# One block for two stages of a language-model tower kernel, fewer DMA issues, and three stores moved to the scalar engine's queue

## The chip, the cores and the metric

The kernel runs on one core of a Trainium2 chip. The metric is the device time of one execution in microseconds (us), as the median of several runs. The core has five instruction streams: TensorE (PE; its weight loads PEld), VectorE (DVE), ScalarE (ACT), GpSimd (POOL) and SyncE (SP). SP computes nothing; it issues transfers, each after the waits that stand before it. ACT and POOL can issue transfers too. All transfers run on the core's 16 DMA engines.

## What is computed

For B = 8 sequences of L = 512 tokens with D = 256 channels, the reference looks up embeddings and adds an attention layer and a mixture-of-experts layer:

```
h = onehot(x) @ embeddings
h = h + attn(layernorm(h))      # linear attention by a weighted delta rule, 16 heads of 16 channels
h = h + ffn(layernorm(h))       # router picks 2 of 8 experts, plus a shared expert

k, q, v = short_conv(x @ W + b, conv); k, q normalised by head; v = silu(v); beta = sigmoid(x @ Wbeta)
per chunk: T = tril(B K^T, -1); inv = (1 + T)^-1; U = inv (V - B W); W += K^T U
           O = Q W_avg * a + Q W * c + T_mat * (Q K^T) U
out = rmsnorm(O) @ Wout + bout
```

All types are float32. The kernel works with chunks of 32 tokens instead of the reference's 64, which gives the same result.

## The kernel before

The program has three stages, each with a block of its own in which every engine has its instruction list. At the end of a block all engines meet.

**First stage** (line 444, the page's 0 to about 597 us): a loop over the 8 sequences b. For each, PE projects and ACT and DVE apply the convolution: for n = 0 to 5, PE writes a bank (L575), ACT writes `cv` and `raw` (L695, L698), DVE adds three taps (L804). Then come the norms, K and Q, gram matrices and masked scores. The results go to DRAM: Q by channels (`qT_dram`, L471, 16 issues), K by tokens (`kk_dram`, L477, 4 issues), the gram matrix in two halves (`n_dram`, L482, 4 issues), beta K and V (`bv_dram`, L486), the scores (`sT_dram`, L494). The gram matrix is loaded back in another layout (`nx`, L491). DVE then inverts it by 62 half steps (L172, L175), laid between its work for the next two sequences, and SP stores the inverse in 8 issues (`store_inverse`, L184).

**Items.** There are 32 items, four tiles of 128 tokens for each sequence. An item goes through PE and ACT in four steps: `apply_inverse` (L288) gives Y and Z by channels, `turn_yz` (L299) turns them, `apply_scores` (L310) sums Y and Z with the scores, `turn_syz` (L320) turns the sums. POOL multiplies the queries by a table and adds the summed Y (`sum_queries`, L271, L276). In iteration b from 3 on, the first stage also works the items of sequence b - 3, placed by hand between its own PE and ACT instructions; so items 0 to 19 lie in the first stage. Items 20 to 31 lie in steps 0 to 3, 5 to 8 and 12 to 15 of the second stage.

SP moves the data of the items: `load_x` (the block-diagonal inverse `xbd`, 4 issues at L225, and `bv_i`, L227), `load_scores` (`sbd`, 4 issues at L234, and `q_i`, L238), `store_y` (L243), `store_rest` (Z and inner products, 4 issues at L251, and the queries, L254). `move_item(r)` issues them in this order:

```
load_x(sp, r + 1); store_y(sp, r); store_rest(sp, r - 1); load_scores(sp, r + 1)
```

`xbd`, `sbd` and `q_i` have one buffer each, so `load_x(r + 1)` waits until item r is solved, and `load_scores(r + 1)` until item r is scored and its queries are scaled.

**Second stage** (line 960, to about 915 us): 32 steps, each a chunk of four sequences. Each step loads Y, Z with inner products, K and queries (`load_step`: L978, L982, L987, L990, double buffered), keeps the state in PSUM, and ends in residual, layernorm, router scores and picks. u (L1155) is copied once in each step. POOL fills the residual rows `h` by gathers (L1012) over rows set to zero (L1019 for the first 4, L1023 for the rest). At its start SP loads weights and indices (L965), for which every other engine waits.

**Third stage** (to the end at 1516.8 us): the experts. The change leaves it as it is.

Of the kernel before, what the change touches and what calls it, by code (L numbers as in the profile page):

```python
# [6 lines left out]
P = 128  # L7
B, L, D = 8, 512, 256
H, DH = 16, 16
C = 32  # L10
# [95 lines left out]
def build(nc, ids, ids_lane, emb, wqkv, wbeta, wout, router, conv_w, qkv_b, bbeta, bout, rms, const, w_in, w_sw, w_out, out,  # L106
# [14 lines left out]
    with ExitStack() as top:  # L121
# [28 lines left out]
        s_nx = tail.enter_context(nc.semaphore("gram_loaded"))  # L150
        s_unit = tail.enter_context(nc.semaphore("unit_ready"))
        s_sub = tail.enter_context(nc.semaphore("vector_chain_inverse"))
        s_inv = tail.enter_context(nc.semaphore("inverse_ready"))
        s_xst = tail.enter_context(nc.semaphore("inverse_stored"))
# [33 lines left out]
        STORES = 16 * (16 + CH + 2)  # L188
# [14 lines left out]
        s_st = tail.enter_context(nc.semaphore("kv_stored"))  # L203
        s_x_in = tail.enter_context(nc.semaphore("item_x_loaded"))
        s_q_in = tail.enter_context(nc.semaphore("item_q_loaded"))
        s_s_in = tail.enter_context(nc.semaphore("item_scores_loaded"))
        s_bv_in, s_y_st, s_zo_st, s_qy_st = ([tail.enter_context(nc.semaphore(f"{n}{i}")) for i in range(2)]
                                                     for n in ("item_bv_loaded", "y_stored", "zo_stored", "queries_stored"))
        T = {n: tail.enter_context(nc.semaphore("item_" + n)) for n in (
# [19 lines left out]
        def load_scores(sp, r):  # L229
# [16 lines left out]
        def store_rest(sp, r):  # L246
            b, t, i = r // TILES, r % TILES, r % 2
            sp.wait_ge(T["z_ready"], r + 1)
            sp.wait_ge(T["inner_ready"], r + 1)
# [7 lines left out]
        def move_item(sp, r, more=True):  # L257
            if more:
                load_x(sp, r + 1)
            store_y(sp, r)  # L260
            if r:
                store_rest(sp, r - 1)
# [60 lines left out]
        def solved_out(act, r, bank):  # L323
# [4 lines left out]
            if r >= 2:  # L328
                act.wait_ge(s_y_st[r % 2], 16 * (r // 2))
            act.activation(y_out[r % 2][:].rearrange("p c n i -> p n c i"), bank[:].rearrange("p (n c i) -> p n c i", n=HQ, c=CH),  # L330
                           ACT.Copy, scale=table("keep_y")).then_inc(T["y_ready"], 1)

        def turned_out(act, r, bank):
# [4 lines left out]
            if r >= 2:  # L338
                act.wait_ge(s_zo_st[r % 2], 16 * CH * (r // 2))
# [17 lines left out]
        with ExitStack() as ctx:  # L357
# [41 lines left out]
            s_ids, s_w, s_zero = (sem(ctx, n) for n in ("ids_in", "weights_in", "h_zeroed"))  # L399
            s_emb = [sem(ctx, f"embedded{i}") for i in range(RING)]  # L400
            s_refill = sem(ctx, "h_refill_zeroed")
            s_pad = sem(ctx, "pad_zeroed")
            s_zero0 = sem(ctx, "zero_ready")
            s_slots = sem(ctx, "slots_zeroed")
            s_chain = sem(ctx, "vector_chain_a")
            s_xhat = sem(ctx, "xhat_ready")
# [1332 lines left out]
```

## Time and profile before

| | us |
|---|---|
| median of 3 runs | 1499.73 (1498.51 to 1503.61) |
| the profiled execution | 1518.6, its span 1516.8 |
| busy in the span: PE, DVE, ACT, POOL | 1179.7, 764.9, 515.8, 388.6 |
| mean granted TensorE clock | 0.874 of full speed |
| transfers of SP's queue | 202944 packets, 194.28 MB |

Busy times are sums over the whole span, over stages with different limits; an engine that is busy for half the span can still set the pace of one stage. The profiled execution is 18.9 us longer than the median.

### The profile page before, as it was taken

What the parts mean: (1) busy time and instruction counts of PE and PEld (TensorE: products, weight loads), DVE (VectorE), ACT (ScalarE), POOL (GpSimd) and SP (SyncE); (2) the same over time, 40 slices, a digit from 0 to 9 for tenths busy, and PEclk for the clock granted to TensorE, in tenths of its full rate; (3) what the DMA queues carried; (4) which work ended last, traced back from release to release, by engine and by line L of the source; (5) the groups of instructions that cost most, each with busy time, mean ns of one, the idle gap of its engine ahead of it and who ended that gap; (6) DMA issues with size and microseconds to landing.
All of it is one profiled execution on the core that took longest, in us unless ns stands there. A gap on an engine that the chain in (4) does not pass through costs nothing. (4 is left out here: it accounts for less than half of the span.)

```text
span 1516.8 us, 28805 instructions
## 1 busy us (share of the span) xinstructions
PE 1179.7 (78%) x10846; PEld 791.1 (52%) x10846; DVE 764.9 (50%) x1707; ACT 515.8 (34%) x1049; POOL 388.6 (26%) x366
## 2 busy tenths in 40 slices
PE   4766456566656561688697987999999999999997
PEld 2543334353535351466475764555666666666664
DVE  4599849586868683567646873221111212121211
ACT  3454245353636360433243332331122222222221
POOL 6100113131202021513226003662022222222222
PEclk9788679777878785867888997999999999999999
DMA  7644566868585968777687747953122323232322
GB/s 269 188 101 134 120 178 142 251 140 248 128 255 121 259 136 235 199 224 224 179 246 225 230 152 278 377 171 103 32 40 46 48 45 49 44 49 43 49 44 31
DMA packets 237366, 228.68 MB, mean 151 GB/s; under 512 B 88980, under 2 KB 177972, under 8 KB 236080
## 3 DMA queue, kind: packets, MB, share of 16 engines
q1 hardware_dynamic: 202944, 194.28, 45.3%
q0 software_dynamic: 16368, 19.96, 7.5%
q10 hardware_dynamic: 17920, 12.59, 2.8%
q8 instruction: 91, 1.49, 0.4%
q14 instruction: 43, 0.35, 0.1%
HBM read 117.39 MB, written 115.62 MB: 154 GB/s over the span
## 5 line engine op out<-in xcount | busy, mean ns | idle before, releaser
L1644 DVE TENSOR_TENSOR hid_all<-p_s,silu 128x512 f32<-128x512 f32 x103 | 71.3, 692 | 378.8 <-PE p_s L1495 249.7
L1694 POOL DMA_INDIRECT out_h<-y_sb,x_in x71 | 110.6, 1558 | 360.9 <-DVE y_sb L1656 343.0
L1552 ACT ACTIVATE silu<-p_m 128x512 f32<-128x512 f32 x103 | 61.5, 597 | 328.0 <-PE p_m L1488 223.4
L804 DVE SCALAR_TENSOR_TENSOR cv<-raw,conv_sb,cv 128x512 f32<-128x512 f32 x144 | 117.5, 820 | 83.6 <-ACT raw L698 81.7
L175 DVE TENSOR_TENSOR xt<-xt,prod 128x62 f32<-128x62 f32 (+15 forms) x248 | 142.0, 572 | 4.3
L172 DVE TENSOR_TENSOR prod<-nx,xt 128x62 f32<-128x62 f32 (+15 forms) x248 | 138.4, 558 | 2.5
L1510 PE MATMUL p_y<-wo,hid_all 128*128 x568 | 134.4, 379 | 0.8 <-ACT hid_all L1569 0.8
L1488 PE MATMUL p_m<-wi,xT_c 128*128 x284 | 133.5, 592 | 0.5 <-ACT xT_c L1565 0.5
L1495 PE MATMUL p_s<-ws,xT_c 128*128 x284 | 133.6, 593 | 0.0
L288 PE MATMUL p_item<-xbd,bv_i 128*32 128x128 f32 x1024 | 46.8, 340 | 108.4 <-issue 39.5
L575 PE MATMUL p_p<-xT,wqkv_sb 128*128 128x512 f32 x192 | 108.6, 705 | 0.7 <-issue 0.7
L1510 PEld LDWEIGHTS p_y<-wo,hid_all 128*128 128x128 f32 x568 | 102.5, 190 | 12.4 <-issue 1.4
L276 POOL TENSOR_TENSOR qy_out<-qy_out,sy_out 128x512 f32<-128x512 f32 x32 | 46.3, 1446 | 219.7 <-ACT sy_out L349 219.7
L271 POOL TENSOR_TENSOR qy_out<-q_i,cst_early 128x512 f32<-128x512 f32 x32 | 38.4, 1201 | 226.7 <-DMA q_i<-q_channels_dram 226.5
L288 PEld LDWEIGHTS p_item<-xbd,bv_i 128*32 128x32 f32 x1024 | 35.6, 135 | 116.7 <-issue 83.9
L629 PE MATMUL p_g<-kqM,kT 32*32 32x128 f32 x2048 | 52.8, 333 | 47.3 <-DVE h L874 26.4
L1684 POOL DMA_INDIRECT slots_in_dram<-rows,slot_of x64 | 62.2, 972 | 46.0 <-ACT rows L1560 31.5
L1488 PEld LDWEIGHTS p_m<-wi,xT_c 128*128 128x128 f32 x284 | 53.9, 190 | 38.4 <-issue 34.8
L1656 DVE COPY y_sb<-p_y 128x256 f32<-128x256 f32 x71 | 30.2, 425 | 85.5 <-PE p_y L1510 84.3
L629 PEld LDWEIGHTS p_g<-kqM,kT 32*32 32x32 f32 x2048 | 40.3, 121 | 59.0 <-issue 57.1
L1495 PEld LDWEIGHTS p_s<-ws,xT_c 128*128 128x128 f32 x284 | 48.5, 190 | 34.4 <-issue 34.4
L1453 PE MATMUL p_m<-xnT_c,wi 128*128 128x512 f32 x128 | 62.0, 608 | 5.3 <-DMA wo<-in_w_out 5.3
(155 smaller groups left out, 2093.9 us busy)
## 6 DMA issues: line engine op xcount, KB each, us to landing
slots_in_dram<-xt SPq DMA_DIRECT2D x18, 520.0 KB
x_in<-slots_in_dram SPq DMA_DIRECT2D x71, 130.0 KB, 2.1
q_channels_dram<-qT SPq DMA_DIRECT2D x128, 64.0 KB
k_tokens_dram<-h SPq DMA_DIRECT2D x32, 256.0 KB
chunk_gram_dram<-h SPq DMA_DIRECT2D x32, 256.0 KB
beta_kv_dram<-h SPq DMA_DIRECT2D x8, 1024.0 KB
nx<-chunk_gram_dram SPq DMA_DIRECT2D x8, 1024.0 KB, 6.3
scores_dram<-h SPq DMA_DIRECT2D x8, 1024.0 KB
```

The costliest lines, as they stand in the source:

```text
L172: ins = dve.tensor_tensor(pr, nx[b % 2][:, m, :, 0:m].rearrange("p e k -> p k e").unsqueeze(3).to_broadcast([P, m, 2, w]), xt[b % 2][:, m, ...
L175: ins = dve.tensor_tensor(kept, kept, pr, ALU.add)
L288: ins = pe.matmul(bank[C * f:C * f + C, n * P:(n + 1) * P], bv_i[r % 2][:, 4 * n + f, :], xbd[:, :, 4 * n + f, :], start=True, stop=True)
L575: ins = pe.matmul(p_p[n % 2][:], wqkv_sb[:, k, p, m * P:(m + 1) * P], xT[:, k, :], start=(k == 0), stop=(k == KH - 1))
L629: ins = pe.matmul(p_g[c * C:(c + 1) * C, g % 4, t % 2, g // 4, :], kT[r, g // 4, tok], kqM[r, g // 4, :, :, tok].rearrange("p w e i -> p ( ...
L804: ins = dve.scalar_tensor_tensor(cv[:, p, m, :], raw[:, p, m, j:j + L], conv_sb[:, p, m, j:j + 1], cv[:, p, m, :], ALU.mult, ALU.add)
L1488: ins = pe.matmul(p_m[n % 2][:], xT[s % 2][:, k, :], wi[:, e, k, :], start=(k == 0), stop=(k == KH - 1))
L1495: ins = pe.matmul(p_s[n % 2][:], xT[s % 2][:, k, :], ws[:, e, k, :], start=(k == 0), stop=(k == KH - 1))
L1510: ins = pe.matmul(p_y[s % 2][:, 0, :], hidT[s % 2][:, f * P:(f + 1) * P], wo[:, e, f, :], start=(f == 0), stop=(f == FK - 1))
L1644: dve.tensor_tensor(dst, p_s[n % 2][:], silu[n % 2][:], ALU.mult).then_inc(S["hid_ready"], 1)
L1684: pool.indirect_dma_start(xs_dram, bass.IndirectOffsetOnAxis(slot_of[:, t, k:k + 1], 0), rows[q][:, k, :], None).then_inc(s_scat[q], 16)
L1694: pool.indirect_dma_start(token_rows, bass.IndirectOffsetOnAxis(x_in[s % X_IN][:, D:D + 1].bitcast(U32), 0), y_sb[s % 2][:], None, compute ...
```

## The change

Five edits:

1. The two first stages share one block. The second stage's weights, indices and the loads of its steps 0 and 1 are issued by SP in the last iteration of the first stage (`start`). The other engines go from one stage into the next, each with waits of its own for what it overwrites. Banks and semaphores are laid out anew for this.
2. Q is stored in 8 issues instead of 16, K in 1 instead of 4, Z with the inner products in 1 instead of 4. The DRAM layouts of the three change with that: Q by head group and channel, K and Z by sequence and token.
3. Y and Z with inner products are stored by ACT, each right behind the ACT instruction that completes it.
4. SP's order changes: in an iteration from b = 2 on, the load of the inverse for the second item of the next iteration stands ahead of the load of `nx` and the store of the scores; the loads for item 0 stand in the middle of iteration 2 instead of at its end.
5. ACT waits for the stores of K alone before it overwrites K, not for all stores of the sequence.

```diff
-    qT_dram = nc.dram_tensor("q_channels_dram", [B, TILES, P, HQ, P], F32, kind="Internal").ap()
-    kk_dram = nc.dram_tensor("k_tokens_dram", [NC_BATCH, B, C, 2 * D], F32, kind="Internal").ap()
+    qT_dram = nc.dram_tensor("q_channels_dram", [B, HQ, P, L], F32, kind="Internal").ap()
+    kk_dram = nc.dram_tensor("k_tokens_dram", [B, L, 2 * D], F32, kind="Internal").ap()
-    zo_dram = nc.dram_tensor("z_and_inner_dram", [NC_BATCH, B, C, 2 * D], F32, kind="Internal").ap()
+    zo_dram = nc.dram_tensor("z_and_inner_dram", [B, L, 2 * D], F32, kind="Internal").ap()
...
-            sp.dma_start(q_i[:], qT_dram[b, t]).then_inc(s_q_in, 16)
+            sp.dma_start(q_i[:], qT_dram[b, :, :, t * P:(t + 1) * P].rearrange("n p l -> p n l")).then_inc(s_q_in, 16)
-        def store_y(sp, r):
+        def store_y(act, r):
-            sp.wait_ge(T["y_ready"], r + 1)
-            sp.dma_start(y_dram[b // GROUP, t * CH:(t + 1) * CH, :, b % GROUP].rearrange("c p x -> p c x"),
+            act.wait_ge(T["y_ready"], r + 1)
+            act.dma_start(y_dram[b // GROUP, t * CH:(t + 1) * CH, :, b % GROUP].rearrange("c p x -> p c x"),
...
-            for c in range(CH):
-                sp.dma_start(zo_dram[t * CH + c, b], zo_out[i][tok(c)].rearrange("p w h d -> p (w h d)")
-                             ).then_inc(s_zo_st[i], 16)
+            act.dma_start(zo_dram[b, t * P:(t + 1) * P], zo_out[i][:].rearrange("p w h d -> p (w h d)")).then_inc(s_zo_st[i], 16)
...
                         if b >= AHEAD:
-                            move_item(sp, r)
+                        if r:
+                            store_queries(sp, r - 1)
+                        load_scores(sp, r + 1)
                             move_item(sp, r + 1)
...
-                        for f in range(4):
-                            for m in range(2):
+                    for n in range(HQ):
                                 for w in range(2):
-                                    sp.dma_start(qT_dram[b, :, f * C + w * DH:f * C + (w + 1) * DH, m::2].rearrange("t d n l -> d n t l"),
-                                                 qT[m * 4 * DH + f * DH:m * 4 * DH + (f + 1) * DH].rearrange("d n (t l) -> d n t l", t=TILES)
-                                                 ).then_inc(s_st, 16)
+                            sp.dma_start(qT_dram[b, n].rearrange("(f w d) l -> w f d l", w=2, d=DH)[w],
+                                         qT[n % 2 * 4 * DH:(n % 2 + 1) * 4 * DH, n // 2]).then_inc(s_st, 16)
...
+                        if half == 0 and b == B - 1:
+                            start_next(sp)
+                        if half == 0 and b == AHEAD - 1:
+                            load_x(sp, 0)
+                            load_scores(sp, 0)
...
+                    if AHEAD - 1 <= b < B - 1:
+                        load_x(sp, r + 5)
                         sp.wait_ge(s_ngst, 64 * (b + 1))
...
                         if b:
-                            act.wait_ge(s_st, b * STORES)
+                        act.wait_ge(s_kst, b * K_STORES)
...
+            def start(sp):
+                sp.wait_ge(first["s_cv"], 6 * B)
                     for dst, src in ((wout_in[:], wout), (router_sb[:], router), (rms_sb[:], rms), (bout_sb[:], bout),
...
+                load_step(sp, 0)
+                load_step(sp, 1)
...
                         sp.dma_start(zo[i][:].rearrange("p w d -> p (w d)"),
-                                     zo_dram[c, b:b + GROUP].rearrange("b i x -> (b i) x")).then_inc(s_zo[i], 16)
+                             zo_dram[b:b + GROUP, c * C:(c + 1) * C]).then_inc(s_zo[i], 16)
...
                             sp.dma_start(kk[i][:].rearrange("p n x -> p (n x)"),
-                                         kk_dram[c, b:b + GROUP].rearrange("b i x -> (b i) x")).then_inc(s_kk[i], 16)
+                                 kk_dram[b:b + GROUP, c * C:(c + 1) * C]).then_inc(s_kk[i], 16)
...
+                pool.wait_ge(s_kst, K_STORES * B)
+                pool.wait_ge(first["s_bv"], 4 * B)
                     pool.memset(h[:, 0:4], 0.0).then_inc(s_hz, 1)
...
+                pool.wait_ge(s_st, STORES * B)
+                pool.wait_ge(first["s_ngst"], 64 * B)
                     pool.memset(h[:, 4:], 0.0).then_inc(s_hz, 1)
...
+                    if s == 0:
+                        pe.wait_ge(first["s_sT"], TILES * B)
                         pe.wait_ge(s_kk[s % 2], 16 * k_loads(s))
```

How SP's list moves, from the store of beta K and V in the iteration of b = 6 on. Each row is an issue (line, destination <- source, the shape of the destination); `h` is the space in which the first stage keeps K, the gram matrix and the scores. Before:

```order
L486 DMA beta_kv_dram<-h 128x4x512
L225 DMA xbd<-chunk_inverse_dram 32x512 x4
L227 DMA bv_i<-beta_kv_dram 128x512
L243 DMA y_channels_dram<-y_out 128x4x128
L251 DMA z_and_inner_dram<-zo_out 32x512 x4
L254 DMA queries_dram<-qy_out 128x4x128
L234 DMA sbd<-scores_dram 32x512 x4
L238 DMA q_i<-q_channels_dram 128x512
L482 DMA chunk_gram_dram<-h 128x8x64 x2
L491 DMA nx<-chunk_gram_dram 128x2048
L494 DMA scores_dram<-h 128x4x512
L225 DMA xbd<-chunk_inverse_dram 32x512 x4
```

In the changed program, from the same store on:

```order
L492 DMA beta_kv_dram<-h 128x4x512
L227 DMA xbd<-chunk_inverse_dram 32x512 x4
L229 DMA bv_i<-beta_kv_dram 128x512
L257 DMA queries_dram<-qy_out 128x4x128
L236 DMA sbd<-scores_dram 32x512 x4
L240 DMA q_i<-q_channels_dram 128x4x128
L483 DMA chunk_gram_dram<-h 128x8x64 x2
L227 DMA xbd<-chunk_inverse_dram 32x512 x4
L229 DMA bv_i<-beta_kv_dram 128x512
L499 DMA nx<-chunk_gram_dram 128x2048
L502 DMA scores_dram<-h 128x4x512
L257 DMA queries_dram<-qy_out 128x4x128
```

The issues for Y and Z are gone, and the second load of `xbd` stands ahead of `nx` and the scores. Earlier in the same iteration the Q stores (L471, in the changed program L474) go from 16 rows with the destination shape 32x4x128 to 8 with 4x16x512.

SP's list in the last iteration of the first stage, in the changed program; the two stages' transfers are now mixed, and K's and Z's loads walk a source of 4 sequences by 32 tokens by 512 numbers:

```order
L966 DMA ids_lane_sb<-in_ids_lane 128x32
L986 DMA zo<-z_and_inner_dram 128x1x512
L992 DMA kk_b<-k_tokens_dram 128x1x512
L982 DMA yy<-y_channels_dram 128x512
L986 DMA zo<-z_and_inner_dram 128x1x512
L992 DMA kk_b<-k_tokens_dram 128x1x512
L995 DMA qq<-queries_dram 128x512
L492 DMA beta_kv_dram<-h 128x4x512
L227 DMA xbd<-chunk_inverse_dram 32x512 x4
L229 DMA bv_i<-beta_kv_dram 128x512
```

Before, the same loads stood behind the end of the block:

```order
L494 DMA scores_dram<-h 128x4x512
L444 UNCONDITIONAL_BRANCH
L961 UNCONDITIONAL_BRANCH
L965 DMA wout_in<-in_wout 128x512
L965 DMA router_sb<-in_router 128x16
L965 DMA rms_sb<-in_rms 128x1
L965 DMA bout_sb<-in_bout 128x256
L965 DMA ids_lane_sb<-in_ids_lane 128x32
L982 DMA zo<-z_and_inner_dram 128x512
L987 DMA kk_b<-k_tokens_dram 128x512
L978 DMA yy<-y_channels_dram 128x512
L982 DMA zo<-z_and_inner_dram 128x512
```

ACT's list at the end of an item, around the start of the convolution of the next sequence. Before:

```order
L346 COPY syz_ch<-p_item 128x512
L349 ACTIVATE sy_out<-p_item,cst_early 128x4x4x32
L354 COPY zo_out<-p_item 128x256
L695 ACTIVATE cv<-p_p,now_b,conv_sb 128x512
L698 ACTIVATE raw<-p_p,qkvb_sb 128x512
```

In the changed program:

```order
L349 COPY syz_ch<-p_item 128x512
L352 ACTIVATE sy_out<-p_item,cst_early 128x4x4x32
L357 COPY zo_out<-p_item 128x256
L252 DMA z_and_inner_dram<-zo_out 128x512
L696 ACTIVATE cv<-p_p,now_b,conv_sb 128x512
```

A store, with a wait for the copy just before it, now stands between the item's last copy and the first output of the convolution.

## Rows read from the trace of the kernel before

**Rows 1.** Windows by stage: us, busy (xinstructions) per engine, clock, DMA share, GB/s

```profile
170.00:252.00 82.00, 43.39 (x639) 31.08 (x638) 60.47 (x117) 36.15 (x65) 9.74 (x7) 0.79 0.61 157
...
484.00:562.00 78.00, 47.94 (x706) 34.86 (x704) 60.72 (x108) 39.02 (x72) 12.71 (x11) 0.82 0.76 192
...
562.00:602.00 40.00, 5.07 (x132) 3.73 (x132) 19.80 (x31) 0.75 (x2) 4.40 (x5) 0.52 0.80 213
...
602.00:761.00 159.00, 115.82 (x1866) 88.97 (x1866) 102.21 (x259) 50.73 (x125) 56.68 (x49) 0.75 0.73 211
...
761.00:803.00 42.00, 37.30 (x676) 29.39 (x675) 18.69 (x70) 21.19 (x53) 14.06 (x14) 0.91 0.81 243
```

**Rows 2.** Waits in order of total, DVE, 170 to 605: total, times, longest

```profile
DVE cv L804 <- ACT raw L698: 71.3, 13, 17.6
...
DVE wout_sb L1236 <- DMA ids_lane_sb<-in_ids_lane: 19.8, 1, 19.8
```

**Rows 3.** Waits, PE, 170 to 610

```profile
PE p_item L288 <- issue: 38.5, 4, 14.1
...
PE p_item L288 <- DMA xbd<-chunk_inverse_dram: 31.4, 4, 8.5
...
PE p_item L288 <- DMA bv_i<-beta_kv_dram: 25.7, 2, 24.5
```

**Rows 4.** Timeline of the last two batches, SP: start, us, issue, [idle <-releaser]

```profile
480.29 11.07 SPq L471 DMA_DIRECT2D q_channels_dram<-qT  x16
...
497.74 0.98 SPq L486 DMA_DIRECT2D beta_kv_dram<-h  x1
...
498.84 3.22 SPq L225 DMA_DIRECT2D xbd<-chunk_inverse_dram  x4
...
512.77 0.46 SPq L494 DMA_DIRECT2D scores_dram<-h  x1
...
513.34 2.11 SPq L225 DMA_DIRECT2D xbd<-chunk_inverse_dram  x4
```

**Rows 5.** Timeline of the last batch, PE and DVE

```profile
505.26 1.94 PE L288 MATMUL p_item<-xbd,bv_i 128*32 128x128 f32 x32 [7.76 <-issue]
...
523.11 1.94 PE L288 MATMUL p_item<-xbd,bv_i 128*32 128x128 f32 x32 [7.41 <-DMA xbd<-chunk_inverse_dram]
...
529.11 0.75 DVE L804 SCALAR_TENSOR_TENSOR cv<-raw,conv_sb,cv 128x512 f32<-128x512 f32 x1 [9.19 <-ACT raw L698]
```

**Rows 6.** Timeline, issues of SP and ACT for an item

```profile
503.10 1.87 SPq L251 DMA_DIRECT2D z_and_inner_dram<-zo_out  x4
...
683.83 0.52 ACTq L1197 DMA_DIRECT2D ffn_input_channels_dram<-xnT  x1
```

**Rows 7.** Timeline of the change of stage, DVE, SP, PE, POOL

```profile
580.20 0.69 DVE L874 TENSOR_TENSOR h<-p_g,cst_early 128x512 f32<-128x512 f32 x1
...
587.91 0.43 SPq L494 DMA_DIRECT2D scores_dram<-h  x1
...
597.06 0.36 SPq L965 DMA_DIRECT2D wout_in<-in_wout  x1
...
602.54 1.19 PE L1040 MATMUL p_u_turn_x<-zo,cst 128*128 128x256 f32 x2 [31.48 <-DMA zo<-z_and_inner_dram]
...
607.91 6.10 POOL L1023 MEMSET h<- 128x7168 f32 x1
...
617.14 0.34 SPq L238 DMA_DIRECT2D q_i<-q_channels_dram  x1
```

**Rows 8.** Timeline of step 3, PE

```profile
646.58 1.93 PE L288 MATMUL p_item<-xbd,bv_i 128*32 128x128 f32 x32 [11.21 <-DMA bv_i<-beta_kv_dram]
```

**Rows 9.** Window of ten late steps, columns as in rows 1

```profile
835.00:893.00 58.00, 55.55 (x1112) 42.20 (x1100) 47.24 (x179) 18.59 (x60) 0.00 (x0) 1.00 0.72 225
```

**Rows 10.** Page, part 2: GB/s in 40 slices

```profile
GB/s 269 188 101 134 120 178 142 251 140 248 128 255 121 259 136 235 199 224 224 179 246 225 230 152 278 377 171 103 32 40 46 48 45 49 44 49 43 49 44 31
```

**Rows 11.** Instructions of L1155, 835 to 900

```profile
L1155 ACT COPY u<-p_u_turn_x x12: 372/373/374, 835.4 to 899.6; 128x256 f32<-128x256 f32 x12
```

More of the change, by code:

```diff
@@ L887, in build @@
-        with ExitStack() as ctx:
+                        if half == 0:
+                            sp.wait_ge(s_bv, b * 4 + 4)
+                            sp.dma_start(bv_dram[b].rearrange("(t p) x -> p t x", p=P),
+                                         bv[:].rearrange("p t h w d -> p t (h w d)")).then_inc(s_st, 16)
+                            if b >= AHEAD:
+                                move_item(sp, r + 3)
+                    if AHEAD - 1 <= b < B - 1:
+                        load_x(sp, r + 5)
@@ new lines, in sync @@
+            def sync(sp):
+                for s in range(NT):
+                    if s >= 2:
+                        load_step(sp, s)
+                    if s == 3:
+                        store_inverse(sp, B - 2)
+                    if s - 1 in item_in:
+                        r = item_in[s - 1]
+                        move_item(sp, r, more=r + 1 < ITEMS and r != BREAK)
+                    if s == 11:
+                        store_inverse(sp, B - 1)
+                        load_x(sp, BREAK + 1)
+                        load_scores(sp, BREAK + 1)
+                    if s == step_of[ITEMS - 1] + 2:
+                        store_queries(sp, ITEMS - 1)
@@ new lines, in gpsimd, with gather, add_bias @@
+            def gpsimd(pool):
+                pool.wait_ge(s_weights, 16 * 5)
+                def gather(n):
+                    pool.indirect_dma_start(h[:, n, :], None, emb, bass.IndirectOffsetOnAxis(ids_sb[:, n:n + 1].bitcast(U32), 0),
+                                            bounds_check=VOCAB - 1, oob_is_err=False).then_inc(s_lane[n % 4], 16)
+                def add_bias(n):
+                    pool.wait_ge(s_lane[n % 4], 16 * (n // 4 + 1))
+                    pool.tensor_tensor(h[:, n, :], h[:, n, :], bout_sb[:], ALU.add).then_inc(s_hb, 1)
+                pool.wait_ge(s_kst, K_STORES * B)
+                pool.wait_ge(first["s_bv"], 4 * B)
+                pool.memset(h[:, 0:4], 0.0).then_inc(s_hz, 1)
+                pool.wait_ge(s_hz, 1)
+                for n in range(4):
+                    gather(n)
+                pool.wait_ge(s_st, STORES * B)
+                pool.wait_ge(first["s_ngst"], 64 * B)
+                pool.memset(h[:, 4:], 0.0).then_inc(s_hz, 1)
+                pool.wait_ge(s_hz, 2)
+                for n in range(NT):
+                    add_bias(n)
+                    if n + 4 < NT:
+                        gather(n + 4)
+                    if n in item_in:
+                        sum_queries(pool, item_in[n])
@@ L960, in build @@
+            return dict(start=start, sync=sync, gpsimd=gpsimd, tensor=tensor, scalar=scalar, vector=vector)
+        with ExitStack() as ctx:
+            first = first_stage(ctx)
+        with ExitStack() as ctx:
+            second = second_stage(ctx)
             with nc.Block() as block:
@@ L993, in _ @@
-                    for s in range(NT):
-                        load_step(s)
-                        if s == 3:
-                            store_inverse(sp, B - 2)
-                        if s - 1 in item_in:
-                            r = item_in[s - 1]
-                            move_item(sp, r, more=r + 1 < ITEMS and r != BREAK)
-                        if s == 11:
-                            store_inverse(sp, B - 1)
-                            load_x(sp, BREAK + 1)
-                            load_scores(sp, BREAK + 1)
-                        if s == step_of[ITEMS - 1] + 2:
-                            store_rest(sp, ITEMS - 1)
+                    first["sync"](sp, second["start"])
@@ L1149, in _ @@
+                    first["tensor"](pe)
+                    second["tensor"](pe)
                 @block.scalar
                 def _(act):
[L1151 to L1161 removed]
@@ L1226, in _ @@
-                    store_xnT(NT - 1)
-                    for i in range(2):
-                        act.wait_ge(s_xn_out[i], 16 * (NT // 2))
-                        act.wait_ge(s_xnT_out[i], 16 * (NT // 2))
+                    first["scalar"](act)
+                    second["scalar"](act)
                 @block.vector
                 def _(dve):
-                    link = Chain(dve, S["chain"], -1)
-                    dve.wait_ge(s_weights, 16 * 5)
-                    for k in range(KH):
-                        dve.tensor_scalar(wout_sb[:, k, :], wout_in[:, k, :], rms_sb[:, 0:1], None, ALU.mult).then_inc(s_wout, 1)
@@ L1338, in build @@
+                    second["vector"](dve)
         tail.close()
```

1544 lines of the change are left out of this document (769 added, 775 removed).

## The prediction, written before the result was known

> **What bounds the kernel now.** I read the windows by stage first, then the waits, then the timeline at the waits found. In the last full batch of the first stage DVE is busy 60.7 of 78 us, PE 47.9 [rows 1]. So DVE sets the pace there where it has work. The list of DVE's waits says when it has none: 71.3 us in front of the taps for ACT's `raw`, in 13 places, 17.6 us of it once [rows 2]. ACT is late because PE stands still in front of `apply_inverse`: 38.5, 31.4 and 25.7 us, by name behind `xbd` and `bv_i` [rows 3]. So a load of an item holds PE, PE holds ACT, and ACT holds DVE.
>
> The timeline of SP shows why these loads are late. For item 16, SP spends 11.07 us on the 16 Q stores, stores beta K and V at 497.74 and comes to `xbd` at 498.84. For item 17 it comes to `xbd` at 513.34, behind 1 MB of `nx` and 1 MB of scores [rows 4]. PE gets the first at 505.26 after 7.76 us and the second only at 523.11, after 7.41 us; DVE then stands 9.19 us [rows 5].
>
> At the change of stage DVE has its last masked scores at 580.9 and next works at 601.2, for the weights (19.8 us) [rows 2, 7]. PE stands 31.48 us. POOL sets `h` to zero only from 607.91, and SP, which has to wait until POOL has scaled the first item's queries behind that, comes to the next loads at 617.14 [rows 7]. From there SP issues nearly without a pause to the `xbd` of step 3, for which PE waits to 646.58 [rows 8]. The late steps are PE's: 55.6 of 58 us [rows 9].
>
> **The change, part by part.** All terms are against the profiled execution, 1518.6 us.
>
> *Loads of items earlier.* The loads of item 0 move from behind the scores of b = 2 to the middle of that batch; that takes nearly all of the 17.6 us away. For the later batches I take item 17. PE would have been free at 523.11 - 7.41 = 515.7, and `xbd`, now issued behind the gram matrix alone, some 6 us earlier, has landed by then. DVE's tap follows `apply_inverse` by 529.11 - 523.11 = 6 us, so it comes at 521.7; DVE has been free since 519.9. Of 9.19 us, 1.8 remain [rows 5]. The load of item 16 waits for DVE's beta K as before (L486, then L225) and gains under 1 us; about 2 us a batch of small waits behind it stay. Left over five batches: 5 x 3.8 = 19 us of the 71.3, so 52 saved. The merged Q, K and Z issues shorten SP's list, by 11.07 / 2 for Q and 1.87 x 3/4 for each Z [rows 4, 6], but at the Q stores SP then only waits for DVE's beta K: nothing more.
>
> *Y and Z on ACT.* An issue with many rows took ACT 0.52 us and SP 1.87 / 4 = 0.47 [rows 6]; the wait for ACT's own copy in front of it adds one or two tenths. Of 8 such in a batch I count two on the way to a `raw`: 5 x 1.2 = 6 us against. In the second stage they lie in ACT's idle time. Behind an issuing ACT waits the next `cv`, and for that DVE. Under a full queue an issue took 3.22 / 4 = 0.8 us [rows 4]; that end is in the last rival.
>
> *One block.* PE and DVE can go on at 581 instead of 602: the first half of step 0 moves by 24 us. But the second half of POOL's zeroing still waits for the scores' landing, and SP waits for POOL. The scores go out at 587.91, and SP comes to the weights at 597.06 [rows 7]; POOL can so start at 597 rather than at 607.91. SP's list is shorter, which brings the scores forward by some 3 us, but four large loads of the second stage now stand in front of them and take this back, and a little more. Since everything up to 646.58 hangs on that chain, I count 10 us, not 24; bounds 6 and 18.
>
> *Merged transfers.* The bytes are the same. Their shape is not: the Q stores have an outermost count of 4, and so has the source of the loads of Z and K in the second stage (4 sequences). No transfer of the kernel before has one under 16. I take it that a transfer is dealt out over the 16 DMA engines by its outermost entries; then these 64 stores and 62 loads run on 4 engines each, and if always on the same ones, these carry the stage. No row shows this, so both ends are priced. If 16 engines share as before, the term is 0. On four engines:
>
> - Late steps, 58 us for ten: 225 GB/s x 5.8 us = 1.31 MB each [rows 9]. Two loads (0.52 MB) on four engines and the rest on 16 give 131 + 49 = 180 KB to a loaded engine. An engine moves 225 / 16 / 0.72 = 19.5 GB/s while busy [rows 9]; in the best slice 377 / 16 = 23.6 [rows 10]. So a step needs 9.2 or 7.6 us, not 5.8. Their packets are of the better kind, so 8.2: 12 steps from 835 on [rows 11] x 2.4 = 29 us (22 to 41).
> - Steps 12 to 15, 42 us: 2.55 MB each, 258 KB to a loaded engine, 10.9 to 13.8 us at 23.6 and 18.8 GB/s [rows 1]. I take 13.2 against 10.5: 11 us (2 to 13).
> - Steps 0 to 11, 159 us: 2.80 MB each, 273 KB, 11.6 to 15.1 us against 13.25 [rows 1]: 8 us (0 to 22). Steps 16 to 19: 2 us (0 to 4).
> - First stage: a batch keeps an engine busy 0.76 x 78 = 59 us, at 192 / 16 / 0.76 = 15.8 GB/s [rows 1]. The Q stores, 1.05 MB, add 196 KB to a loaded engine, 8.3 to 12.4 us: 68 to 72. The batch after the first term is about 69 us, so this just fits or costs up to 3: 4 us in all.
>
> The Trainium skill ("DMA: Bandwidth & Descriptors", section "Why a DMA increments its semaphore by 16 and not by 1") states a rule of this kind: the number of engines is the largest one up to 16 that divides the slowest count of both sides, and these are always the lowest-numbered. By it the sum below holds; with 16 engines the same sum would be about -65. No run here shows it yet.
>
> Sum: -52 + 6 + 4 = -42 for the first stage, -10 for the change of stage, +50 for the second: **-2 us**, 1516.6 in the profiled execution. The median stands at 1499.73 / 1518.6 = 0.9876 of it: **1498 us**.
>
> **The rivals.**
>
> 1. *Faster, 16 engines for every shape.* For it: every row so far moves at a rate of all engines. Against it: four outermost entries can't be dealt to 16 without cutting them. Then first stage -46, change of stage -18, second 0 or a little less: -65, 1453.6, so 1435.
> 2. *Faster, four engines that keep up.* The low ends: the loaded engines run at 23.6 GB/s, since their packets are of 2 KB. First stage -46, change -14, second +24: -36, so 1463.
> 3. *Slower, the loads of Z and K in the second stage bind.* Place: L986 and L992. At 18 to 19.5 GB/s the late steps take 9.2 us, the steps with items 13.8 and 15.1: +80. In the first stage the loaded engines are full, loads of items queue behind Q stores, and only 30 of its gain stay; 6 remain at the change. +44, so 1543. It decides as soon as the second stage loses over 52 us, with the late steps over 8.3 us.
> 4. *Slower, ACT's stores.* At 0.8 us each plus the wait, and all 64 on the way, 45 us more than counted: 1543. Against it: ACT is busy half of the first stage's batch.
>
> **How the numbers follow.** A measurement tells about 0.3% (4.5 us) from no change. Forecast 0.40, rival 1 0.13, rival 2 0.20, rival 3 0.22, rival 4 0.05. The forecast's own terms spread by some 18 us about 1498, which gives faster 0.16, within 0.3% 0.11, slower 0.13. Faster: 0.13 + 0.20 + 0.16 = 0.49; the same: 0.11; slower: 0.22 + 0.05 + 0.13 = 0.40. The range has to reach both sides, to 1436 and 1542; it leaves out half of rival 1 and the upper half of rivals 3 and 4. The forecast's own range is 1475 to 1520.
>
> **What would show it.** In the profile after: DVE's wait for `raw` at about 20 instead of 71 us, none of them over 4; a batch of 69 to 71 us; PE's gap at the change of stage under 12 us, and SP's `q_i` of item 21 some 10 us earlier against the end of the first stage. Packets of Q stores must be 2 KB, and a late step must take about 8.2 us with PE waiting for `zo` or `kk_b`. Late steps of 5.8 us mean rival 1, and the second stage's gain is then 18; of over 8.5 us, rival 3. If the waits in front of `apply_inverse` remain at 7 us, my first term is wrong. A long busy stretch of ACT's queue between item copies and `cv` means rival 4.

## The result, and the profile after

The changed kernel is **slower**: four runs gave 1512.7, 1517.6, 1519.7 and 1527.1 us, median 1518.64, against 1501.67 for the kernel before; the ratio is 1.0109 with a 95% interval of 1.0076 to 1.0142. One of the four runs of the kernel before took 1864.11 us and is left out of the ratio; the median of the other three is the 1499.73 of the first table. By the medians of four that is 17 us more, about 1%, where 1498 was forecast. The time lies in the stated range, but the likeliest case had the wrong side.

The profiled execution of after took 1512.7 us (the shortest of the four), its span 1510.2. Against the 1518.6 us of the first profile of the kernel before it looks faster. So the kernel before was profiled a second time (experiment b0, 1503.5 us). The table sets all three side by side. The first stage's end is the end of DVE's last masked scores (L874), the next four columns are starts of u (L1155 before, L1166 after), the last is the rest of the execution's time.

| us | end of first stage | u of step 4 | step 12 | step 20 | last (31) | behind it |
|---|---|---|---|---|---|---|
| before, first profile | 580.9 | 659.6 | 760.9 | 835.4 | 899.6 | 619.0 |
| before, second (b0) | 576.6 | 655.3 | 751.6 | 819.4 | 885.8 | 617.7 |
| after | 538.2 | 626.2 | 726.4 | 811.1 | 894.3 | 618.4 |
| after less b0, by part | -38.4 | +9.3 | +3.9 | +16.9 | +16.8 | +0.7 |

The first stage gives back 38 us, everything behind it takes 48. Against the first profile the same parts are -42.7, +9.3, -1.1, +10.2, +19.0 and -0.6, together -5.9. Two stretches of that execution are long. One is the start: ACT's first `xT` copy of b = 3, before any item is worked, comes at 170.4 us in the first profile, at 159.1 in b0 and at 159.2 in after. So 11.2 of the 42.7 us lie ahead of b = 3, where b0 and after are alike, and are not the change's; from that copy to the end of the first stage it is 410.4 us in the first profile, 417.5 in b0 and 378.9 in after, a gain of 31.5 or 38.6. The other is steps 12 to 20, 74.5 us against b0's 67.8, where the change costs.

**The first stage.** The list of waits of after, DVE, 170 to 605 us (total, times, longest):

```profile
DVE norm L836 <- ACT norm L723: 17.8, 5, 5.0
DVE cv L804 <- ACT raw L699: 17.5, 13, 3.6
```

The wait for `raw` was 71.3 us with a longest of 17.6 [rows 2]; it is 17.5 now, none over 3.6. A wait for `norm` (8.0 us before) has grown. Why is not shown: it is 16.0 in f3, which has SP's old order, 15.7 in f2, which stores Y and Z from SP, and 8.1 in g1, which has neither the one block nor the merged stores. The waits of PE for an item (170 to 610 us) beside those of [rows 3]:

```profile
PE p_item L290 <- DMA xbd<-chunk_inverse_dram: 41.3, 5, 13.2
...
PE p_item L290 <- issue: 7.9, 1, 7.9
...
PE p_item L290 <- DMA bv_i<-beta_kv_dram: 5.2, 2, 3.0
```

95.6 us have become 54.4, and the 13.2 among them lie in the first step of the second stage.

**The change of stage.** SP's timeline of after (start, us, issue):

```profile
537.87 2.59 SPq L995 DMA_DIRECT2D qq<-queries_dram  x1
540.50 0.52 SPq L492 DMA_DIRECT2D beta_kv_dram<-h  x1
541.14 4.29 SPq L227 DMA_DIRECT2D xbd<-chunk_inverse_dram  x4
...
546.42 4.16 SPq L236 DMA_DIRECT2D sbd<-scores_dram  x4
...
551.09 3.84 SPq L483 DMA_DIRECT2D chunk_gram_dram<-h  x2
558.73 0.35 SPq L499 DMA_DIRECT2D nx<-chunk_gram_dram  x1
559.14 0.44 SPq L502 DMA_DIRECT2D scores_dram<-h  x1
...
563.94 1.72 SPq L236 DMA_DIRECT2D sbd<-scores_dram  x4
577.02 0.38 SPq L240 DMA_DIRECT2D q_i<-q_channels_dram  x1
```

and POOL's:

```profile
567.82 6.07 POOL L1033 MEMSET h<- 128x7168 f32 x1 [24.58 <-DMA scores_dram<-h]
...
575.90 1.10 POOL L273 TENSOR_TENSOR qy_out<-q_i,cst_early 128x512 f32<-128x512 f32 x1
```

The scores are issued at 559.14, 21 us behind DVE's end; before it was 7 us behind (587.91 against 580.9 [rows 7]). POOL waits for their landing to 567.82, 30 us behind that end. Before it was 27, though the scores went out so much earlier: POOL then came to this point only behind the change of block, the weights and four gathers. SP stands from 565.7 to 577.0 for the queries that POOL scales next. PE starts step 0 at 540.5, 62 us earlier than before, and then waits: u of steps 0 to 4 took 55.8 us before and takes 84.4.

**The late steps.** The window of eleven late steps of after; columns as in [rows 9], which answers to it (us, busy of PE, PEld, DVE, ACT, POOL, granted clock, DMA share, GB/s):

```profile
811.00:894.00 83.00, 71.83 (x1235) 52.53 (x1232) 53.58 (x198) 21.18 (x66) 0.00 (x0) 0.88 0.52 168
```

A step takes 7.6 us on the mean (83.2 / 11), not 5.8, and the DMA engines are busy 52% on the mean over all 16, not 72%. The waits of ACT and PE in that window:

```profile
ACT xnT L1204 <- DMA ffn_input_channels_dram<-xnT: 13.5, 7, 2.6
```

```profile
PE p_u_turn_x L1049 <- ACT xnT L1204: 8.9, 7, 1.9
```

In this window PE never waits for `zo` or `kk_b` themselves. ACT waits to overwrite `xnT`, whose store is behind, and PE for ACT; PE's idle time is 11 us of 83. The granted clock is 0.88 where it was 1.00, so the matmuls are also slower (PE is busy 6.5 us in a step, and was 5.6).

### The profile page after: what moved, and what is told of

Read it like the earlier page. It is cut to its first block and busy times, and to the rows that moved or that the text cites. A ratio compares the mean times of both kernels' runs of the same rounds, so it can differ in the third digit from the quotient of the medians.

```text
span 1510.2 us, 28640 instructions
## 1 busy us (share of the span) xinstructions
PE 1194.3 (79%) x10846; PEld 803.2 (53%) x10846; DVE 767.6 (51%) x1707; ACT 518.1 (34%) x1049; POOL 391.4 (26%) x366
## 5 line engine op out<-in xcount | busy, mean ns | idle before, releaser
L1686 DVE TENSOR_TENSOR hid_all<-p_s,silu 128x512 f32<-128x512 f32 x103 | 71.3, 692 | 378.3 <-PE p_s L1537 249.7
L172 DVE TENSOR_TENSOR prod<-nx,xt 128x62 f32<-128x62 f32 (+15 forms) x248 | 141.5, 570 | 2.5
L577 PE MATMUL p_p<-xT,wqkv_sb 128*128 128x512 f32 x192 | 104.2, 681 | 0.7 <-ACT xT L691 0.7
L290 PE MATMUL p_item<-xbd,bv_i 128*32 128x128 f32 x1024 | 43.0, 320 | 64.2 <-DMA xbd<-chunk_inverse_dram 43.3
L273 POOL TENSOR_TENSOR qy_out<-q_i,cst_early 128x512 f32<-128x512 f32 x32 | 42.1, 1314 | 187.3 <-DMA q_i<-q_channels_dram 187.2
L1530 PEld LDWEIGHTS p_m<-wi,xT_c 128*128 128x128 f32 x284 | 53.9, 190 | 38.4 <-issue 34.8
L290 PEld LDWEIGHTS p_item<-xbd,bv_i 128*32 128x32 f32 x1024 | 32.5, 127 | 72.6 <-DMA xbd<-chunk_inverse_dram 49.3
```

What stands on the lines that cost most here:

```text
L172: ins = dve.tensor_tensor(pr, nx[b % 2][:, m, :, 0:m].rearrange("p e k -> p k e").unsqueeze(3).to_broadcast([P, m, 2, w]), xt[b % 2][:, m, ...
L290: ins = pe.matmul(bank[C * f:C * f + C, n * P:(n + 1) * P], bv_i[r % 2][:, 4 * n + f, :], xbd[:, :, 4 * n + f, :], start=True, stop=True)
L577: ins = pe.matmul(p_p[n % 2][:], wqkv_sb[:, k, p, m * P:(m + 1) * P], xT[:, k, :], start=(k == 0), stop=(k == KH - 1))
L1530: ins = pe.matmul(p_m[n % 2][:], xT[s % 2][:, k, :], wi[:, e, k, :], start=(k == 0), stop=(k == KH - 1))
L1686: dve.tensor_tensor(dst, p_s[n % 2][:], silu[n % 2][:], ALU.mult).then_inc(S["hid_ready"], 1)
```

## Experiments

All ratios are to the kernel before, run on the same chip; its median was 1505.01 us beside b0 to e3, 1515.27 beside f1 to f4 and 1515.02 beside g1 to g4. So kernels of different groups are compared by their ratios. f2, f3 and f4 are edits of e1, which was not run beside them; f1 stands in for it there. g3 and g4, the same two kernels as e1 and f1 on one chip, differ by 1 us.

### b0: the kernel before, profiled again

> The kernel before, unchanged, profiled again. The profile that the prediction used took 1518.6 us where the timed runs took 1498.5 to 1503.6. Theory A: that execution was a long one by chance and a second profile comes near 1500 us; then the sum has to be made against 1500, and the comparison of the two profiles (1518.6 and 1512.7) hides some 19 us of loss. Theory B: a profiled execution of this kernel is always about 19 us longer, then it comes to 1515 to 1522 again and the ratio to the other runs of before is 1.000 within 0.003.

Measured: 1505.18, ratio 1.0007 (0.9986 to 1.0028), the profiled execution 1503.5 us. Theory B falls: a profiled execution is not longer as such. The first profile is long by 4.3 us in the first stage (11.3 at the start, 7.0 of them back behind it) and by 9.5 from step 4 to 31 (table above). That it was so by chance, as theory A has it, is not shown. The same kernel has medians of 1515.27 and 1515.02 us on two other chips, with single runs up to 1520.65. The first `xT` copy of b = 3 comes at 169.5 to 171.9 us in all eight profiles taken there, as in the first profile, and at 159.1 to 161.4 in those of b0, e1, e2 and e3. So the first profile looks like one of another chip; on which it was taken is not on record.

### e1: loads of Z and K as four loads of one sequence

```
-                sp.dma_start(zo[i][:]..., zo_dram[b:b + GROUP, c * C:(c + 1) * C]).then_inc(s_zo[i], 16)
+                for n in range(GROUP):
+                    sp.dma_start(zo[i][lane(n)]..., zo_dram[b + n, c * C:(c + 1) * C]).then_inc(s_zo[i], 16)
```

and the same for `kk`; PE waits for 16 * GROUP.

> The changed kernel, with each load of Z and of K for the second stage as four loads of one sequence (32 rows) instead of one with an outermost count of 4; 186 more issues of SP. Theory (these 62 loads run on four DMA engines and carry the second stage): late steps go from 7.2 us and more back to 5.8, the second stage from first to last u goes from 352 to 300 to 315 us, and the time to 1470 to 1485. Rival (the second stage is long for SP's order, the stores from ACT or the early start): late steps stay over 7 us and the time at 1510 to 1525, or goes up for the added issues.

Measured: 1477.03 us, ratio 0.9833 (0.9786 to 0.9879). Against the changed kernel's 1.0109 that is 2.8%, some 41 us less, for 186 more issues. The window of late steps in e1, then its DMA issues in that window (KB each, median us from issue to landing), then those of after, 811 to 894 us:

```profile
790.00:855.00 65.00, 61.75 (x1237) 47.40 (x1237) 53.71 (x202) 20.80 (x67) 0.47 (x1) 1.00 0.72 215
```

```profile
qq<-queries_dram SPq DMA_DIRECT2D x11, 256.0 KB, 3.7
yy<-y_channels_dram SPq DMA_DIRECT2D x10, 256.0 KB, 3.8
...
ffn_input_channels_dram<-xnT ACTq DMA_DIRECT2D x11, 128.0 KB, 3.3
```

```profile
yy<-y_channels_dram SPq DMA_DIRECT2D x10, 256.0 KB, 6.7
...
qq<-queries_dram SPq DMA_DIRECT2D x10, 256.0 KB, 9.2
...
ffn_input_channels_dram<-xnT ACTq DMA_DIRECT2D x11, 128.0 KB, 7.1
```

The late steps are back at 5.8 to 5.9 us (64.6 for eleven), the clock at 1.00. The transfers shown are the same in both kernels, and none has an outermost count of 4. They land in about half the time once the loads of Z and K are dealt out. The reading: a transfer over all engines has landed only when the last of them is done, and in after four of them are busy with Z and K.

### g1: the kernel before, with only the memory order of Z and K changed

```
-    kk_dram = ...("k_tokens_dram", [NC_BATCH, B, C, 2 * D], ...)
-    zo_dram = ...("z_and_inner_dram", [NC_BATCH, B, C, 2 * D], ...)
+    kk_dram = ...("k_tokens_dram", [B, L, 2 * D], ...)
+    zo_dram = ...("z_and_inner_dram", [B, L, 2 * D], ...)
```

Stores and loads use the new addresses, in the same number of issues.

> The kernel before, with the order of Z and of K in memory as the change has it (sequence, then token), and nothing else: the same issues, bytes and packets, but the 62 loads of the second stage walk a source of 4 x 32 x 512, where before it was one run of 128 rows. Theory (by that shape they run on four DMA engines): the load increments its semaphore 4 times and not 16 times, late steps go from 5.8 to 7.0 us and more, and the time rises by 30 to 45 us over the kernel before. Rival (in the changed kernel something else made the steps long): within 5 us of the kernel before.

Measured: 1548.02 us, ratio 1.024 (1.017 to 1.0309): 36 us (26 to 47) from the memory order alone. The page's row of SP's queue (packets, MB, share), first of the kernel before (b0), then of g1:

```profile
q1 hardware_dynamic: 202944, 194.28, 46.0%
```

```profile
q1 hardware_dynamic: 202200, 194.28, 44.2%
```

The bytes are the same; 744 packets are gone, which is 62 loads x 12. (The expectation had said "the same packets".) The semaphore events in the traces tell what they were. In b0 a Z load has 16 events from the DMA side (508 on record for 32 loads), in g1 5 (151 for 32; some are missing), in the late steps one within 1.0 us of the issue and four late. The Z load issued at 855.83 has them at 856.77 and at 864.38 to 864.77. So four engines report a landing where 16 did.

The packets show that these are the same four engines for Z and K. While a Z and a K load of one step are both on their way (from 1.5 us behind the K load's issue to Z's landing, 63 us in all between 845 and 925), exactly four packets are in flight in 31% of the time; on eight engines it would mostly be eight or more. Over the whole late window it is 31% in g1 and 26% in after (811 to 894), against 1% in b0 (820 to 885) and 2% in e1. A Z load lands after 9.0 us (median) and a K load after 11.3, where b0 has 2.7 and 3.6; in after it is 6.7 and 9.3.

The late steps take 6.2 to 8.1 us, 7.3 on the mean. This is the cleanest proof: nothing of the order, the blocks or the queues differs. The place in memory does differ, but e1 reads the same places with 16 engines and has late steps of 5.9 us.

### e2 and e3: the Q stores on 16 engines

e2 gives the changed kernel the 16 Q stores of before (partitions outermost, pieces of 512 B) and the Q layout that goes with them; e3 is e1 and e2 together.

> The changed kernel, with the Q stores alone as before: 16 issues of 512 B pieces in a batch, partitions outermost. Theory (four engines for the Q stores cost the first stage little): the batch stays at 70 to 73 us, the time within 6 us of 1518.6. Rival (the four-engine Q stores hold up the items' loads behind them): the batch falls to 68 us or less, the waits for xbd go from 41 us to under 25, and the time falls by 12 us or more.

> Both edits, so no transfer has an outermost count of 4. Theory: the gain of the loads and that of the Q stores add up, 1468 to 1485 us. If the four-engine shapes were no matter, 1510 to 1530.

Measured: e2 1515.11 us, ratio 1.0072 (1.0035 to 1.011); e3 1476.55, ratio 0.9805 (0.9773 to 0.9838). e3 and e1 differ by 0.5 us in their medians and by 0.3% in their ratios, e2 and after by 0.4% in their ratios; the intervals overlap in both pairs. So the Q stores on four engines cost 0 to 6 us. The batches of e2 do not become shorter (70.9 to 75.2 us, 69.9 to 73.5 in after). Its waits for `xbd` fall as the rival said, from 41.3 to 22.0 us, but the wait of the same instruction that is named "issue" grows from 7.9 to 23.6. Whether the gains of e1 and e2 add up is within the noise.

### f3: SP's order of before, in e1

The lines that move `load_x(r + 5)` ahead of `nx` and item 0 to the middle of b = 2 are taken back.

> e1, with SP's order of the kernel before: the x of a batch's first item loaded at the start of its own batch, behind nx and the scores of the last, and the loads of item 0 behind the scores of b = 2. One block, ACT's stores and the merged stores stay. Theory (the first stage's gain of 42 us comes from the order): DVE's waits for raw are back at 65 to 75 us, and the time rises by 35 to 50 us, to 1512 to 1527. Rival (fewer issues or ACT's stores made the loads early): it rises by under 20 us.

Measured: 1524.22 us, ratio 1.0051 (1.0029 to 1.0072), against 0.9834 for f1 on that chip: 33 us by the ratios, 35 by the medians. The first stage ends at 579.5 us, and DVE's waits (170 to 590 us) show why:

```profile
DVE cv L800 <- ACT raw L695: 62.7, 15, 16.2
DVE norm L832 <- ACT norm L719: 16.0, 5, 4.6
```

The order alone makes the gain of the first stage. It was expected at 35 to 50 us and is just at or under the lower edge. Without it one block, merged stores and ACT's queue, with every load on 16 engines, leave a kernel 0.5% slower than before.

### f2: Y and Z stored from SP again, in e1

```
     def move_item(sp, r, more=True):
...
+            store_y(sp, r)
             if r:
+                store_zo(sp, r - 1)
                 store_queries(sp, r - 1)
```

> e1, with the stores of Y and of Z and inner products (one issue each) put back into SP's queue, where the kernel before had them. Theory (the stores from ACT cost the first stage 6 to 10 us, seen as DVE's wait for norm of 18 instead of 8 us): that wait is back at 8 us and the time falls by 4 to 9 us, to about 1470. Rival (they relieve SP, whose list sets when item loads go out): the waits for xbd grow and the time rises by 5 us or more.

Measured: 1494.53 us, ratio 0.9851 (0.9819 to 0.9884), beside 0.9834 (0.9803 to 0.9864) for f1. Its waits of DVE:

```profile
DVE cv L806 <- ACT raw L701: 30.7, 15, 4.1
...
DVE norm L838 <- ACT norm L725: 15.7, 5, 4.5
```

The theory falls: the wait for `norm` hardly changes (17.0 in f1), so ACT's issues do not make it, and the wait for `raw` is 8 us longer than f1's 22.4. The time is 5.8 us over f1's by the medians and 0.2% by the ratios, whose intervals overlap. So the stores from ACT cost nothing that can be measured and may gain a little.

### f4: the early start taken away, in e1

`start_next(sp)` moves from the middle of b = 7 to behind its scores.

> e1, with the early start taken away: SP issues the second stage's weights and the loads of steps 0 and 1 behind the scores of the last batch. Theory (the early start is worth nothing, since POOL waits for the scores, which its 24 issues hold up): u of step 0 comes 15 to 20 us later, that of step 4 within 4 us of e1's, the time within 5 us of 1477. Rival (the early start is worth the 24 us by which step 0 moves): 1495 or more.

Measured: 1493.13 us, ratio 0.9861 (0.983 to 0.9893). u of step 0 comes at 565.2, 18 us behind the first stage's end (547.4), where in e1 both fall together; yet u of step 4 comes 79.6 us behind that end, in e1 81.2. The time is 4.4 us over f1's by the medians. The intervals overlap and leave room for about 11: the early start of step 0, 24 us by the prediction's count, is worth 4 us or nothing, at most some 11.

The same run shows what holds the scores up. Their issue in f4, where the first stage ends at 547.4, and then in e1, where it ends at 541.8:

```profile
551.77 0.43 SPq L500 DMA_DIRECT2D scores_dram<-h  x1
```

```profile
559.69 0.43 SPq L502 DMA_DIRECT2D scores_dram<-h  x1
```

That is 4.4 and 17.9 us behind that end. So the issues of the next stage in front of them cost the scores some 13 us.

### f1, g3, g4, g2: POOL's wait for the scores

f1 lets POOL zero lanes 0 to 7 first (the K quarter of `h`) and wait for the scores only at lane 4:

```
-                pool.memset(h[:, 0:4], 0.0).then_inc(s_hz, 1)
+                pool.memset(h[:, 0:8], 0.0).then_inc(s_hz, 1)
...
                 for n in range(NT):
                     add_bias(n)
+                    if n == 4:
+                        pool.wait_ge(s_st, STORES * B)
+                        pool.wait_ge(first["s_ngst"], 64 * B)
+                        pool.memset(h[:, 8:], 0.0).then_inc(s_hz, 1)
+                        pool.wait_ge(s_hz, 2)
```

g4 is f1 again, g3 is e1 again, and g2 is f1 with K in memory as before, so that each K load is one issue on 16 engines.

> e1, with POOL's order at the change of stage alone altered: its first memset takes the K quarter of h (lanes 0 to 7), and the wait for the scores with the memset of the rest stands behind the sums of the first items, at lane 4. In e1 SP stands from 566.2 to 578.5 us for POOL's scaled queries, which stand behind that wait. Theory (the chain scores, POOL, SP takes back what the early start gives): SP's stand of 12 us goes, the time from DVE's last masked scores to the u of step 4 falls from 82 to under 72 us, and the time from 1477 to 1463 to 1470. Rival (the DMA engines are full there, or xbd is late by its own chain): 1472 to 1480.

> e1 again, on the chip of g1, g2 and g4: 0.983 of the kernel before, as in its first run (0.9786 to 0.9879).

> f1 again, beside e1 on one chip. In f1's trace the time from DVE's last masked scores to the u of step 4 was 74.5 us, in e1's 81.9, but the two ran on different chips. Theory: 4 to 8 us under g3. Rival: the steps behind give it back, within 3 us of g3.

> e1 with POOL's order of f1, and K in memory as before (four stores in a batch, each load of a step one issue on 16 engines again): 90 issues of SP fewer in the second stage and 24 more in the first. Theory (SP's list is part of the chain of the early steps, and f1's edit is worth 7 us to step 4): the fastest of all, 5 to 12 us under g3. Rival (DMA engines are full there and the issues are hidden): within 4 us of g3.

Measured: f1 1488.76, ratio 0.9834 (0.9803 to 0.9864); g3 1488.21, 0.982 (0.9765 to 0.9875); g4 1487.23, 0.9828 (0.9771 to 0.9884); g2 1483.55, 0.9805 (0.9756 to 0.9854). SP's stand of 12 us is gone in f1:

```profile
563.92 0.34 SPq L499 DMA_DIRECT2D nx<-chunk_gram_dram  x1
564.30 0.43 SPq L502 DMA_DIRECT2D scores_dram<-h  x1
...
568.55 2.43 SPq L236 DMA_DIRECT2D sbd<-scores_dram  x4
571.02 0.44 SPq L240 DMA_DIRECT2D q_i<-q_channels_dram  x1
```

and the time does not move. What the edit gives up to step 4 goes by step 12 (from the first stage's end):

| | to step 4 | to step 12 | step 12 to 31 |
|---|---|---|---|
| before, two profiles | 78.7, 78.7 | 180.0, 175.0 | 138.7, 134.2 |
| g3 (e1) | 82.8 | 177.9 | 140.2 |
| g4 (f1) | 71.6 | 176.5 | 142.4 |
| f4 (late start) | 79.6 | 179.6 | 140.0 |
| after | 88.0 | 188.2 | 167.9 |
| g1 | 81.3 | 186.0 | 158.4 |

With the loads on 16 engines step 12 comes 175 to 181 us behind the first stage's end in ten of the eleven profiles there are, whatever the first steps do (170.5 in g2's). g4 is 1 us under g3, so the rival of f1 and g4 holds. What binds in between was not taken apart. The trace shows only that PE waits 10 to 13 us for `zo` of step 12 in g3, g4 and after (9.7 and 10.0 before, too), and that SP has issued `chunk_inverse_dram` of the last sequence (L184, 8.2 to 8.9 us) and a further item's loads in front of it.

One kernel's profiles differ here by as much as the edits do: from step 12 to 31 e1 took 132.9 us and g3, the same kernel, 140.2; the difference lies in steps 12 to 20 (68.3 and 76.1), for steps 20 to 31 take 64 to 65 us in every profile with the loads on 16 engines but b0's (66.4).

g2 is faster than both kernels, 1.95% under before. Its lead over e1 is 5 us beside g3 and within the intervals, between its theory (5 to 12) and its rival (within 4); e3 has the same ratio. Its step 12, some 7 us earlier than elsewhere with fewer issues of SP, speaks for the theory, but it is one profile.

## Why the prediction was right and wrong

**The first stage: mechanism right, size 4 to 10 us too good.** -42 was forecast for it. It is -42.7 against the profile that was used, but 11.2 of this lie ahead of the batches with items, so the agreement is luck: the batches gave 31.5 us against that profile and 38.6 against b0, and f3 puts the order at 33 to 35. DVE's wait for `raw` was to fall to about 20 us with none over 4, and is 17.5 with 3.6; a batch was to take 69 to 71 us, and takes 70 to 74 (ACT's `xT` copies, L691, start at 159.2, 232.7, 304.6, 377.9 and 447.8). f3 shows that it is the order. Of the 17.6 us at the first batch with items, of which nearly all was to go, the batch gained 8.1 (81.6 to 73.5). Of the two costs against it, ACT's +6 was not there (f2), and the Q stores' +4 is within 0 to 6 (e2). The wait for `norm`, which the prediction did not have, took 10 us back.

**The change of stage: the step that failed.** "I count 10 us, not 24; bounds 6 and 18". It cost 9.3 us. The mechanism was named: SP's large loads in front of the scores take back what its shorter list gives, "and a little more". That term was put at next to nothing, and it measured 14 us: the scores went out 20.9 instead of 7.0 us behind DVE's end. The 11 issues of the next stage took SP from 530.04 to 540.50, 10 us, and the item's `xbd` and `sbd` and the second half of the gram matrix behind them took it 12.3 us instead of 6.2; f4 shows that moving the next stage's issues back gives 13 us. So the 11 us by which POOL was to start sooner were gone, and 3 more. PE's gap at the step was 14.4 us and not under 12, and SP's `q_i` of item 21, expected 10 us earlier against the end of the first stage, came 38.8 us behind it, where it had been 36.2. The bounds left a loss out without a reason for it. Not all of the 9.3 is SP's order: with the loads on 16 engines u of step 4 comes 80.3 to 83.0 us behind the end (e1, e3, f2, f3, g3), 2 to 4 us later than before and not 9.3, so the rest seems to belong to the shape of the loads. Of that the prediction had about 3 us here, four twelfths of its +8 for steps 0 to 11, so it stood at -7 for this part and not at -10. The split is rough, for e2 has that shape and 83.7. And f4, f1 and g4 show more: up to step 12 an early start or a shorter chain gave nothing that can be measured, so the lower bound of 6 was hardly to be had either.

**The second stage: mechanism right, sizes off on the lighter side.** The transfers with an outermost count of 4 run on four engines; g1's 12 missing packets and four late semaphore events for each load show the count, and e1 and g1 the price in the whole time: 41 and 36 us. By the rule of the Trainium skill ("DMA: Bandwidth & Descriptors", section "Why a DMA increments its semaphore by 16 and not by 1"), the largest number up to 16 that divides the slowest count of both sides, 4 is what should come, and the trace agrees. That it is always the same engines, the lowest-numbered, that section of the Trainium skill also states. The traces have no engine's number, but Z and K share theirs (four packets in flight with both loads on their way, in 31% of that time in g1), and transfers over all engines land in 6.7 and 9.2 instead of 3.8 and 3.7 us. Term by term (forecast; against the profile used; against b0): late steps +29; 19.0; 16.8. Steps 12 to 19 +13; 10.2; 16.9. Steps 0 to 11 +8; -1.1; 3.9 for steps 4 to 11. So +50 was 28 or 38 from step 4 on. A late step took 7.6 us, the lower of the two prices worked out. By the prediction's estimate of 180 KB a step, a loaded engine then moves 180 KB / 7.6 us = 23.7 GB/s, the rate of the profile's best slice [rows 10]. 8.2, between the two, was taken; the rate to take was that of an engine without a gap. And the waiting engine was not the one named: not PE for `zo`, but ACT for its own store, which shares the engines.

**The sum.** -42 - 10 + 50 = -2 was forecast. Against the profile that was used the parts are -42.7 + 9.3 + 28.1, with -0.6 behind them: -5.9, which looks near, and would be +5.3 without the 11.2 at the start. Against b0 they are -38.4 + 9.3 + 37.6 + 0.7 = +9.2. The medians say +17: after's own profile is its shortest run, 5.9 us under its median, and b0's is 1.8 over the median of before (9.2 + 5.9 + 1.8 = 16.9). So against b0 the first stage was 4 us too good, the change of stage 19 too good, and the second stage 12 too dear; the last hid part of the others. The ratio 0.9876 of median to profile was laid over all parts alike, but b0 shows no such ratio: of the first profile's 15 us, 11 lie at the start and 10 between steps 4 and 31, and 7 come back in between. It made the forecast look sound against the profile. The sign came from the change of stage: with the 9.3 measured there in place of -10 the prediction's own sum is +17.

**The rivals.** 1 and 4 are out (16 engines by g1's count; ACT's stores by f2). 2, four engines that keep up, had the right price for the late steps, and 3 named the right side, slower, but by a price of +80 in the second stage that no run shows. What happened is a fifth case: the forecast's mechanisms, with a change of stage that costs instead of giving.

## What to carry to other kernels

Before two issues are merged into one, look at the outermost count of both sides: one issue with a count of 4 cost this kernel more than three further issues of SP do, and its price shows at other transfers too, as late landings on queues that were not touched. An earlier start of a stage is worth only what the last release on its way allows; move it alone (f4) before it is counted. And profile the kernel before again beside the runs that it is compared with: two profiles of it were 15 us apart here, as much as the effect.

## What had not been expected

- The slow steps of after show no wait for the slow loads. The rows name ACT's store of `xnT`, whose landing took 7.1 us, and 3.3 in e1.
- The average DMA share fell, from 0.72 to 0.52, while transfers became the limit. A mean over 16 engines hides four full ones: fewer than four packets are in flight in only 6% of the late window of after.
- The granted clock in the late steps was 0.88 with 11 us of gaps in 83, and 1.00 with about 3 us in 65 (e1). So of 1.8 us that a step lost, 1.0 went to slower matmuls (PE busy 6.5 against 5.6 us) and 0.8 to waiting.
- A Q store with 2 KB packets on four engines held SP 1.1 us (8.77 us for 8 in the batch at 440 us), one with 512 B on 16 engines 0.7 (11.24 for 16 in b0): half the issues saved a fifth of the time. Bytes, piece size and number of engines all differ between the two, so which of them costs is open.
